# Softmax in a vision transformer layer: the row maximum subtracted on VectorE, not by products on TensorE

## What is computed

```python
q = q * rsqrt(norm(q, axis=1) + EPS)       # axis 1: over the heads
k = k * rsqrt(norm(k, axis=1) + EPS)
dots = einsum('bhid,bhjd->bhij', q, k)
scores = softmax(dots / scale[:, None, None], axis=-1)
out = einsum('bhij,bhjd->bhid', scores, v)
...
h = layernorm(h + attn(h))
h = layernorm(h + ffn(h))
```

## Time and profile before

| | |
|---|---|
| median of 3 runs | 139.73 us (139.38 to 139.88) |
| the profiled execution | 139.37 us |
| its span in the profile | 137.6 us |
| granted TensorE clock, mean | 0.994 |
| TensorE busy | 128.9 us (94%) |
| VectorE busy | 97.4 us (71%) |
| ScalarE busy | 78.7 us (57%) |
| GpSimd busy | 77.3 us (56%) |

### The profile page before, as it was taken

One profiled execution on the slowest core, in us unless ns is written; L12 is line 12 of the kernel. 1 busy time (PEld: TensorE's weight loads), 2 busy tenths in 40 slices (PEclk: granted clock), 3 DMA queues, 4 the chain that ended last, 5 costly groups with the idle time before them and its releaser, 6 DMA issues. The chain is left out here.

```text
span 137.6 us, 3992 instructions
## 1 busy us (share of the span) xinstructions
PE 128.9 (94%) x1564; PEld 119.8 (87%) x1565; DVE 97.4 (71%) x267; ACT 78.7 (57%) x152; POOL 77.3 (56%) x89
## 2 busy tenths in 40 slices
PE   6999899999999999999999999986999999999960
PEld 2779899999889889999989989976999998998950
DVE  0019489837868959447778886898888774788853
ACT  3048589989854458488768631541445445333761
POOL 7302238961278998998752664689934332344600
PEclk9999999999999999999999999999999999999997
DMA  4999954630022222522490068400001655000022
GB/s 128 325 401 406 405 183 138 210 133 0 9 76 53 67 67 57 159 62 80 151 323 27 0 144 198 102 0 0 0 0 37 155 140 122 2 5 0 2 59 70
DMA packets 8987, 15.47 MB, mean 112 GB/s; under 512 B 1224, under 2 KB 5896, under 8 KB 8968
## 3 DMA queue, kind: packets, MB, share of 16 engines
q1 hardware_dynamic: 8968, 15.22, 35.3%
HBM read 9.96 MB, written 0.44 MB: 76 GB/s over the span
## 5 line engine op out<-in xcount | busy, mean ns | idle before, releaser
L523 POOL TENSOR_TENSOR reg_r<-reg_p,reg_r 128x324 fp32r<-128x324 f32 (+1 forms) x23 | 18.6, 810 | 20.5 <-ACT reg_r L759 20.4
L457 POOL TENSOR_TENSOR reg_w<-stage,reg_w 128x768 fp32r<-128x768 f32 x12 | 22.3, 1871 | 7.8 <-ACT reg_w L587 5.4
L759 ACT ACTIVATE reg_r<-reg_p 128x324 fp32r<-128x324 f32 (+1 forms) x23 | 10.2, 444 | 13.7 <-DVE reg_p L1142 13.5
L1344 PE MATMUL ps<-reg_r,reg_w 128*128 128x324 f32 (+1 forms) x48 | 15.1, 315 | 2.2 <-DVE reg_p L1142 2.2
L750 ACT ACTIVATE ps<-ps,sm 128x252 f32<-128x252 f32 (+1 forms) x21 | 9.7, 464 | 11.1 <-PE ps L1348 10.8
L1345 PE MATMUL ps<-reg_r,reg_w 128*128 128x324 f32 (+1 forms) x48 | 14.2, 295 | 0.0
L1347 PE MATMUL ps<-reg_r,reg_w 128*128 128x324 f32 (+1 forms) x48 | 14.2, 295 | 0.0
L1346 PE MATMUL ps<-reg_r,reg_w 128*128 128x324 f32 (+1 forms) x48 | 14.2, 295 | 0.0
L1348 PE MATMUL ps<-reg_r,reg_w 128*128 128x324 f32 (+1 forms) x48 | 14.2, 295 | 0.0
L1107 DVE TENSOR_SCALAR ps<-ps,bup 128x252 f32<-128x252 f32 (+1 forms) x21 | 10.7, 510 | 3.1 <-PE ps L1348 3.0
L493 POOL TENSOR_TENSOR reg_q<-reg_q,rnorm 128x432 f32<-128x432 f32 x7 | 8.9, 1275 | 6.4 <-ACT rnorm L665 6.4
(11 more groups left out here) (207 smaller groups left out, 393.3 us busy)
## 6 DMA issues: line engine op xcount, KB each, us to landing
reg_x<-xw_in SPq DMA_DIRECT2D x5, 416.0 KB, 6.0
stage<-w_gu_a SPq DMA_DIRECT2D x4, 384.0 KB, 4.0
stage<-w_gu_b SPq DMA_DIRECT2D x4, 384.0 KB, 3.4
reg_r<-reg_x SPq DMA_DIRECT2D x24, 54.0 KB
stage<-w_qkv_a SPq DMA_DIRECT2D x3, 384.0 KB, 7.8
stage<-w_qkv_b SPq DMA_DIRECT2D x3, 384.0 KB, 8.1
stage<-w_down SPq DMA_DIRECT2D x3, 384.0 KB, 3.7
stage<-wrow SPq DMA_DIRECT2D x8, 126.0 KB, 2.4
```

Of the source, the lines that this page charges most:

```text
L457: nc.gpsimd.tensor_tensor(dst[:, 1, :], raw, f(dst[:, 0, :]), ALU.subtract).then_inc(s_wlop, 1)
L523: nc.gpsimd.tensor_tensor(acts[:, n % NACT, 1, 0:w], act_f[:, n % 4, 0:w], f(acts[:, n % NACT, 0, 0:w]), ALU.subtract).then_inc(s_alo, 1)
L759: nc.scalar.activation(acts[:, n % NACT, 0, 0:w], act_f[:, n % 4, 0:w], ACT.Copy).then_inc(s_ahi, 1)
L1344: mm(out_ap, w_a(0), x[:, 0, cols], start=True, stop=False)
```

## The change

The maximum is no longer rounded (`mx`, plain fp32). subtract_max(u) goes from TensorE's queue to VectorE's, directly behind row_max(u): it adds the negated maxima, broadcast along the 36 keys, to the scores in PSUM and writes the result into the unit's slot in SBUF. It takes over the wait for p_transpose(u-3), which last read the slot. exps(u) works in place in the slot. What waited for exps to free a PSUM bank (scores, row_max, h1_transpose) now waits for the subtraction. p_transpose(0) takes over the wait for the constants.

```diff
-        mx_r = sb("mx_r", [128, 2, H], f32r)
+        mx = sb("mx", [128, 2, H])
...
                 act.wait_ge(s_sub, u + 1)
-                if u >= 3:
-                    act.wait_ge(s_pt, u - 2)
-                b = s_bank(u)
-                nc.scalar.activation(slots_of(u, slice(0, LANES)).rearrange("p (b h) j -> p b h j", b=2),
-                                     ps[0:LANES, b:b + 2, 0:6 * SEQ].rearrange("p b (h j) -> p b h j", h=6),
-                                     ACT.Exp).then_inc(s_e, 1)
+                nc.scalar.activation(slots_of(u, slice(0, LANES)), slots_of(u, slice(0, LANES)), ACT.Exp).then_inc(s_e, 1)
...
+            def subtract_max(u):
+
+                dve.wait_ge(s_mx, u + 1)
+                if u >= 3:
+                    dve.wait_ge(s_pt, u - 2)
+                b = s_bank(u)
+                nc.vector.tensor_tensor(slots_of(u, slice(0, LANES)).rearrange("p (b h) j -> p b h j", b=2),
+                                        ps[0:LANES, b:b + 2, 0:6 * SEQ].rearrange("p b (h j) -> p b h j", h=6),
+                                        mx[0:LANES, u % 2, :].rearrange("p (b h) -> p b h", b=2).unsqueeze(3)
+                                        .to_broadcast([LANES, 2, 6, SEQ]), ALU.add).then_inc(s_sub, 1)
...
             row_max(0)
+            subtract_max(0)
             q_norm(2)
...
                 if k + 1 < NU:
                     row_max(k + 1)
+                    subtract_max(k + 1)
...
-                    pe.wait_ge(s_e, u - 1)
+                    pe.wait_ge(s_sub, u - 1)
...
-            def subtract_max(u):
-
-                bank = s_bank(u)
-                if u == 0:
-                    pe.wait_ge(s_const, 1)
-                pe.wait_ge(s_mx, u + 1)
-                for b in range(2):
-                    last = mm(ps[0:LANES, bank + b, 0:6 * SEQ].rearrange("p (h j) -> p h j", h=6), ident_r[0:LANES, 0:LANES],
-                              mx_r[0:LANES, u % 2, 6 * b:6 * b + 6].unsqueeze(2).to_broadcast([LANES, 6, SEQ]),
-                              start=False, stop=True, skip_group_check=True)
-                last.then_inc(s_sub, 1)
```

More of the change, by code:

```diff
@@ L978, in row_max @@
                 if u >= 2:
-                    dve.wait_ge(s_e, u - 1)
+                    dve.wait_ge(s_sub, u - 1)
                 b = s_bank(u)
-                nc.vector.reduce_max(mx_r[0:LANES, u % 2, :].rearrange("p (b h) -> p b h", b=2),
+                nc.vector.reduce_max(mx[0:LANES, u % 2, :].rearrange("p (b h) -> p b h", b=2),
                                      ps[0:LANES, b:b + 2, 0:6 * SEQ].rearrange("p b (h j) -> p b h j", h=6),
                                      X, negate=True).then_inc(s_mx, 1)
+            def subtract_max(u):
[7 more added lines that the diff above has]
+                                        .to_broadcast([LANES, 2, 6, SEQ]), ALU.add).then_inc(s_sub, 1)
             def row_sum(u):
@@ L1202, in _ @@
             row_max(0)
+            subtract_max(0)
             q_norm(2)
             row_max(1)
+            subtract_max(1)
             row_sum(0)
@@ L1209, in _ @@
             row_max(2)
+            subtract_max(2)
             row_recip(1)
@@ L1455, in scores @@
                             last = mm(ps[64 * img:64 * img + n, bank + b, c:c + SEQ], qk[rows, m, t:t + n],
-                                      qk[rows, NP + m, t:t + SEQ], start=(i == 0 and r == 0), stop=False,
+                                      qk[rows, NP + m, t:t + SEQ], start=(i == 0 and r == 0), stop=(i == 2 and r == 1),
                                       skip_group_check=True)
                 last.then_inc(s_s, 1)
-            def subtract_max(u):
-                bank = s_bank(u)
-                if u == 0:
-                    pe.wait_ge(s_const, 1)
-                pe.wait_ge(s_mx, u + 1)
-                for b in range(2):
-                    last = mm(ps[0:LANES, bank + b, 0:6 * SEQ].rearrange("p (h j) -> p h j", h=6), ident_r[0:LANES, 0:LANES],
-                              mx_r[0:LANES, u % 2, 6 * b:6 * b + 6].unsqueeze(2).to_broadcast([LANES, 6, SEQ]),
-                              start=False, stop=True, skip_group_check=True)
-                last.then_inc(s_sub, 1)
             def p_transpose(u):
@@ L1477, in p_transpose @@
                     pe.wait_ge(s_ptev, u)
+                if u == 0:
+                    pe.wait_ge(s_const, 1)
                 pe.wait_ge(s_p, u + 1)
@@ L1525, in h1_transpose @@
                 if g < 2:
-                    pe.wait_ge(s_e, NU - 1 + g)
+                    pe.wait_ge(s_sub, NU - 1 + g)
                 pe.wait_ge(s_h1, 2 * g + 2)
@@ L1642, in _ @@
             v_proj(2, (1,))
-            subtract_max(0)
             scores(1)
             v_proj(3, (0,))
-            subtract_max(1)
             scores(2)
@@ L1650, in _ @@
             for k in range(2, NU - 1):
-                subtract_max(k)
                 scores(k + 1)
@@ L1658, in _ @@
                     project(k - 4)
-            subtract_max(7)
             h1_transpose(0)
```

## The result

The changed kernel takes 142.93 us (median of 4 executions, 141.84 to 143.42), the kernel before 139.56 us beside it: 1.024 times as long (95% interval 1.019 to 1.029). Forecast were 142.0 and a range of 140.3 to 143.4. A ratio here leaves out executions more than 1.5% above the kernel's fastest; the medians count them. The profiled execution of the changed kernel is one of 143.42 us, with a span of 141.6 us; about 1.4 us of it goes with a fall of TensorE's clock, which only some executions have (told of with the warming runs).

What follows compares the result with a forecast made beforehand. Two nearly equal chains, TensorE's and GpSimd's, both fed by VectorE, were taken as the bound. Shifts of +1.65 at probs(0), +2.4 at probs(2), +1.9 at project(1) and +2.4 at project(2) gave 142.0 us, range 140.3 to 143.4.

Steps and rivals of the forecast that it cites:

- The prices: Each subtraction takes 0.60 us on VectorE, 0.62 us in its queue; exps from SBUF takes 0.56 us against 0.53.
- That is the whole gain there can be: TensorE loses 16 products in eight units, 2.8 us in all, if it waits for nothing else.
- Step 1, the start: At the softmax start q_norm(2) comes late, w_lo(6) goes first and holds it: +1.65 us at probs(0).
- rival 2: No missed turn at the start, q_norm(2) costs only its 0.62: about +1.0, 140.7 us; chance 0.15.
- Step 2: To probs(2): subtractions 2 and 3 add 1.24 us, q_norm(4) waits 0.5 less; total shift +2.4 us.
- Step 3: GpSimd's run to root(0): idle time before probs(4) and root(0) absorbs some, leaving +1.9 us at project(1).
- Step 4: To project(2): subtraction(7) stands before ln1(1) and adds 0.47 us, total +2.4 us.
- After 65 us: Behind the softmax part everything hangs on what came before, so the 2.4 us carries to the end.
- 1, TensorE as the bound: TensorE's queue bounds the kernel and gets its full 2.8 us: 137.0 us; chance 0.08.
- 3: VectorE's idle time in the expert part absorbs the shift, or TensorE's gain balances it: 139.8 us; chance 0.07.
- 4, a subtraction shut out: GpSimd also holds up subtractions, about 0.6 us in at least four of eight cases: 144.4 us; chance 0.06.
- 5, the clock: TensorE idling between 40 and 67 us drops its clock, up to 3.6 us more: 145 us; chance 0.02.

Runs made afterwards that it cites:

- warming runs: Extra TensorE products on a scratch tile before project(1) and project(2), added to the changed kernel: 142.25 and 142.56 us; with ln1(1) ahead of row_max(7) too: 142.11 us.
- one-operand run: Changed kernel with q_norm of units 2 to 7 replaced by a maximum reading one SBUF operand: 140.24 us, 1.003 of the kernel before.
- repetition: The changed kernel, unaltered, measured and profiled once more: 142.46 us, 1.025 of the kernel before; span 140.4 us.
- reversed order: Changed kernel with ln1(1) ahead of row_max(7) and its subtraction instead of behind them: 143.0 us, 1.024 of the kernel before.
- without q_norm: q_norm's multiplication left out for units 2 to 7, in the changed kernel (140.93 us) and in the kernel before (139.14 us).
- row-bias profile: Kernel before without the products or a subtraction; exps takes one negated maximum per row as bias: 139.03 us, 0.994 of the kernel before.
- two maxima: Kernel before, its products kept, with a second row maximum per unit added on VectorE: 142.66 us, 1.022 of the kernel before.
- q_norm(4) early: Changed kernel with q_norm(4) ahead of v_evac(3) in VectorE's queue: median 142.84 us, 1.010 of the kernel before.

## Why the prediction came out

**Range and sign.** 142.93 us is inside 140.3 to 143.4 and on the side given 0.82, 0.9 us above the point. In the profile without a loss of clock the change costs 2.8 us of span, where the sum said 2.4. That the sum came so near is in part luck: two errors in it cancelled (steps 1 and 2).

**The prices.** The subtraction (0.608 us against 0.60) and exps (0.56) held. "That is the whole gain there can be", 2.8 us for 16 products, is true as a bound and far from the value: 0.6 to 0.8 us where nothing is added.

**Step 1, the start, was wrong.** "w_lo(6) goes first, unheld": q_norm(2) had its turn although w_lo(6) had started 0.31 us earlier; +0.45 at probs(0) instead of +1.65. By two of its own signs the prediction was wrong here: q_norm(2) was short, 0.60 us and not about 2, and probs(0) ended at 44.66, before 45. w_lo(6) was to go back from 2.20 to 1.83 us and went up to 2.60; the one-operand run, where it takes 1.83, has probs(0) at 43.70 as the repetition at 43.71, so that hold costs nothing. That q_norm(2) keeps its turn was rival 2's premise. Its figure, 140.7 us, did not follow from it, because it took no missed turn later on. With the start of rival 2 the right sum was: +0.45 at the start, 1.24 for subtractions 2 and 3, and 0.78 more for q_norm(4) (1.80 against 1.02), 2.47 us. Some 0.2 us less were measured at probs(2), 2.25, since v_evac(3), between reciprocal(1) and q_norm(4), follows its predecessor sooner than before (0.14 us behind its start, not 0.30) and is shorter (0.90 against 0.96).

**Step 2: the total right, a term wrong.** +2.4 at probs(2) was forecast and +2.25 measured. But "arriving later it finds less to wait for: -0.5" had the wrong sign. q_norm(4) arrived later and lost its turn: +0.8. Two errors of 1.2 and 1.3 us cancelled, by luck. The mechanism named, a q_norm that misses its turn and holds up the reciprocal behind it, is the one that carries the loss; I had put it at the wrong instruction.

**Step 3.** +1.9 at project(1) forecast; 61.66 - 59.57 + 0.22 = 2.3 measured. The idle time of 0.64 us before probs(4) was to go; it grew to 0.92, because q_norm(6) lasted 0.94 us longer, which the sum did not have.

**Step 4.** +0.47 forecast from project(1) to project(2), 0.57 measured (2.88 - 2.31). The reversed order gives 0.92 us at project(2) and only 0.2 in the span.

**After 65 us.** "I carry the 2.4 to the end" held: what is there at project(2) is there in the span within 0.1 us, in three pairs (0.8 and 0.8; 2.05 and 2.0; without q_norm 0.93 and 0.9). It doesn't hold where the order behind is changed: with ln1(1) first 0.92 us at project(2) became 0.2. What bounds that stretch then was not traced.

**The rivals.** 1, TensorE as the bound: the products were worth 0.6 to 0.8 us, not 2.8, even without a subtraction. 3 fell with the last point. 4, a subtraction shut out: it took 0.61 us all eight times, also beside GpSimd's k_norm(3) (44.63 to 45.73, the subtraction at 44.96) and k_norm(5). 5, the clock: some loss, in two of the four executions of the result, of 1.4 us and not of 3.6; the median there is 0.5 us above that of the repetition. The Trainium skill ("TensorE: Matmul & The Clock Gate", "HAM oscillation — how this bites in real kernels") has idle gaps lead to a slow clock; the counts, 10 of 22 against 1 of 18, agree in direction, but the row-bias profile, where the clock fell behind waits of at most 0.37 us, speaks against gaps as the only cause. Why it falls in one execution and not in another of the same program stays open.

**What I left open and was decided.** That the exclusion, and not the length of the queue alone, carries 2.0 of the 2.8 us is shown by the run with one operand. A longer queue is what makes q_norm arrive at a bad moment, as the run with two maxima shows; what decides a turn stays open.

## What to carry to other kernels

Before work is moved to an engine with idle time, look for its instructions that another engine can hold up, and count what is queued behind them: here 0.6 us of added work per unit, less what the removed products gave back, cost 0.8 us in all where nothing was held, and 2.8 us where two held operations lost their turns. An instruction that is sometimes held is worth giving one SBUF operand less. Moving it to a place where the other engine is idle freed q_norm(4) here (0.58 us), but in the profile taken the next one lost two turns instead. And price the gain as well: 2.8 us of products off a full TensorE gave 0.6 to 0.8 us, since a second chain, nearly as long, then kept TensorE waiting for ln1.

## What the runs showed of the hardware

**Who gets the turn does not follow from whose recorded start is first.** The Trainium skill ("SBUF — State Buffer", "Who interferes with whom") lets the instruction that starts first keep the other out for its whole length. Here, with q_norm (two SBUF operands) against GpSimd's tensor_tensor:

| q_norm | queued, against GpSimd's instructions | outcome |
|---|---|---|
| (2), changed | 0.31 us behind the start of w_lo(6) | not held; w_lo(6) held until its end |
| (2), two maxima | 0.17 us behind that start | the same |
| (4), changed | 0.26 us before the end of probs(1) | k_norm(4) goes first, 1.80 us |
| (4), two maxima | 0.30 us before it | the same, 1.84 us |
| (4), before | 0.55 us before it | q_norm first, 1.02 us |
| (4), row bias | 0.75 us before it | q_norm first, 1.21 us |
| (6), before and changed | 0.8 and 1.75 us before the end of w_lo(7) | probs(3) goes first, then q_norm: 2.16 and 3.10 us |
| (6), q_norm(4) early | 0.37 us before the end of w_lo(7) | probs(3), then k_norm(6) first: 2.79 us |

I know no rule that fits all eight rows, and no run varied the distance by itself; this stays open. The rule's core, that the two do not run side by side and that an operation with one SBUF operand isn't concerned, agrees with these runs: k_norm, w_lo and probs keep 1.10, 1.83 and 0.91 us beside subtractions and maxima.

**What remains at the end of a hold was nearly the same each time.** A held w_lo of 1.83 us ends 1.69 us after q_norm's end, in the earlier trace rows, in the changed kernel and with two maxima (42.71 - 41.02). A held q_norm of 0.55 us ends 0.45 to 0.47 us after GpSimd's instruction. That is 0.14 us less than the whole operation for w_lo, and 0.08 to 0.10 for q_norm.
